# Seams between the two stages of a four-layer spectral network: copies inside SBUF in place of the way through DRAM, no barriers, and group loads one pair earlier

## What is computed

```python
h = einsum('bhwi,ic->bhwc', x, fc0_w) + fc0_b          # then channels first
for l in range(4):
    xf = rfft2(h)
    top = einsum('bixy,ioxy->boxy', xf[:, :, :16, :16], w1[l])
    bot = einsum('bixy,ioxy->boxy', xf[:, :, -16:, :16], w2[l])
    sc = irfft2(of)                                    # of: top and bot in a spectrum of zeros
    y = sc + einsum('bihw,oi->bohw', h, pw_w[l]) + pw_b[l]
    y = (y - mean) * rsqrt(var + eps) * gamma[l] + beta[l]   # mean and var over images and pixels
    h = gelu(y)
h = gelu(h @ fc1_w + fc1_b); out = h @ fc2_w + fc2_b   # per pixel
```

## Time and profile before

| | us |
|---|---|
| median of 3 runs | 4336.68 (4324.19 to 4337.49) |
| profiled execution | 4346.47 |
| its span | 4344.7 |
| TensorE busy | 3227.5 (74%) |
| VectorE, ScalarE busy | 2415.4 (56%), 2244.2 (52%) |
| DMA | 798.68 MB, mean 184 GB/s |

### The profile page before, as it was taken

How to read it: one execution, slowest core, us unless ns; L and a number is a source line. 1 busy time by engine, 2 the same in 40 slices (tenths; PEclk the granted TensorE clock), 3 DMA queues, 4 the chain that set the end, 5 groups by cost and what they waited for, 6 DMA issues and landing times. The chain is left out here.

```text
span 4344.7 us, 119303 instructions
## 1 busy us (share of the span) xinstructions
PE 3227.5 (74%) x52804; PEld 1863.9 (43%) x52804; DVE 2415.4 (56%) x2474; ACT 2244.2 (52%) x2644; POOL 173.2 (4%) x249
## 2 busy tenths in 40 slices
PE   6758888885577677757577776755999996659777
PEld 4544444444444344435344343444444442543432
DVE  4545555554477677646577676744333332554556
ACT  3545566654466556546456555644666664222321
POOL 2013100000000000000000000000010102000000
PEclk8879999997799889878899888987999998669688
DMA  8857666667768878787678787887343331002042
GB/s 287 308 150 186 173 155 157 172 188 281 242 181 242 248 218 260 209 282 263 214 220 252 216 239 242 245 290 257 120 163 148 142 121 32 1 19 61 1 102 66
DMA packets 172143, 798.68 MB, mean 184 GB/s; under 512 B 31177, under 2 KB 37649, under 8 KB 122286
## 3 DMA queue, kind: packets, MB, share of 16 engines
q1 hardware_dynamic: 160796, 776.18, 58.8%
q0 software_dynamic: 7936, 13.65, 1.0%
q10 hardware_dynamic: 2898, 1.17, 0.1%
HBM read 448.68 MB, written 342.23 MB: 182 GB/s over the span
## 5 line engine op out<-in xcount | busy, mean ns | idle before, releaser
L828 PEld LDWEIGHTS bank<-fb,arena 64*64 64x64 f32 x16384 | 555.7, 196 | 540.1 <-issue 484.1
L828 PE MATMUL bank<-fb,arena 64*64 64x128 f32 x16384 | 619.7, 289 | 196.5 <-issue 140.7
L1045 ACT ACTIVATE arena<-bank 128x1024 f32<-128x1024 f32 x384 | 383.5, 1023 | 638.7 <-PE bank L973 423.7
L845 DVE TENSOR_TENSOR arena<-bank,arena 128x1024 f32<-128x1024 f32 x384 | 467.2, 1217 | 411.4 <-PE bank L828 408.8
L837 DVE STREAM_TRANSPOSE arena<-bank 128x1024 f32<-128x1024 f32 x256 | 318.8, 1245 | 535.7 <-PE bank L818 535.6
L1088 DVE STREAM_TRANSPOSE arena<-arena 128x1024 f32<-128x1024 f32 x384 | 458.3, 1212 | 134.2 <-ACT arena L1035 132.2
L818 PE MATMUL bank<-arena,ga 64*64 64x256 f32 x4096 | 308.8, 413 | 300.0 <-DMA arena<-spec_out 242.0
L973 PE MATMUL bank<-arena,wst 64*64 64x512 f32 x3072 | 414.7, 620 | 17.1 <-issue 11.1
L1052 ACT ACTIVATE arena<-arena 128x1024 f32<-128x1024 f32 x384 | 403.2, 1050 | 0.3
L1038 ACT ACTIVATE arena<-arena,shift,scale 128x1024 f32<-128x1024 f32 x256 | 316.3, 1236 | 129.2 <-DVE arena L845 127.0
L818 PEld LDWEIGHTS bank<-arena,ga 64*64 64x64 f32 x4096 | 167.3, 142 | 430.9 <-issue 359.3
(11 more groups left out here) (238 smaller groups left out, 3647.1 us busy)
## 6 DMA issues: line engine op xcount, KB each, us to landing
y_dram<-arena SPq DMA_DIRECT2D x384, 512.0 KB, 8.2
arena<-y_dram SPq DMA_DIRECT2D x96, 2048.0 KB
arena<-spec_in SPq DMA_DIRECT2D x32, 2048.0 KB, 10.0
spec_out<-arena SPq DMA_DIRECT2D x128, 512.0 KB, 8.2
arena<-in_w_modes SPq DMA_DIRECT2D x28, 2048.0 KB, 14.2
arena<-spec_out SPq DMA_DIRECT2D x112, 512.0 KB, 10.4
spec_in<-arena SPq DMA_DIRECT2D x96, 512.0 KB, 7.9
spec_in<-arena SPq DMA_DIRECT2D x8, 2048.0 KB, 12.5
```

The source lines that it names most:

```text
L828: mm = pe.matmul(hpx(bank[2 * s + i][CHAN[v], :])[:, :, j * S:(j + 1) * S], a2[p % 2][CHAN[i], :, v, 4 * T + j], hpx(fb2[CHAN[i], :]), sta ...
L845: dve.tensor_tensor(chunk(p, T), slot(s), chunk(p, T), ALU.add).then_inc(y_added, 1)
L1045: act.activation(chunk(p, T), slot(NEXT_SLOT[T]), ACT.Copy).then_inc(evicted, 1)
```

## The change

1. `load_piece(n)` becomes `load_piece(n + 1)`, with one piece more ahead of the loop: each quarter of a group is issued one pair earlier.
2. Mix to fused stage: the last chunk of group 0 is no more loaded from `spec_out` behind a barrier, but copied from `m_sb` into `grp[0]` by four DMAs of 64 KB, ahead of the chunk's stores. `turn` of the last half comes ahead of `cross`, and ScalarE's squares of that half wait for it. The arithmetic of the batch norm is cut: sums behind `rows` of pair 0's first half, variance and scale around `turn_rows` of pair 0.
3. Fused stage to mix: spectra of chunks 0 and 1 are loaded without the last group (1792 KB each) once their buffers are free: chunk 0 in SyncE's turn of pair 31, chunk 1 at the end. Their last group comes from `xs` by four DMAs of 64 KB each. The rotated copies of chunks 0 and 1 are made in two pieces, seven groups and the last.
4. The seven `phase_end` between the stages go; single waits on semaphores stand for them. The buffers of the mix are laid out so that `xs` lies on `m_sb[1]`.

```diff
@@ mix
+        def load_last_group(sp, c, src):
+            for v in range(2):
+                for ro in range(2):
+                    to = ro * C + v * HB
+                    sp.dma_start(s_sb[c][to:to + HB, NG - 1], src(c, v, ro)).then_inc(s_last_group, 16)
...
             def store(c):
                 sp.wait_ge(mixed_turned, (l * NCH + c) * 4 + 4)
...
+                for t in range(4):
+                    row = t % 2 * C + t // 2 * HB
+                    if c == NCH - 1:
+                        sp.dma_start(grp[0].rearrange("p (c v) b o -> p c (v b o)", v=2)[row:row + HB, c],
+                                     m_sb[c % 2][t * HB:(t + 1) * HB, 0].rearrange("p v x -> p (v x)")).then_inc(grp_loaded[0], 16)
...
-            for c in range(3):
-                load(c)
+            if first:
+                for c in range(2):
+                    load_spectra(sp, c, slice(0, NG - 1))
+                    if c > 0:
+                        sp.wait_ge(s_last_group, 64)
+                    load_last_group(sp, c, lambda c, v, ro: spec_in[c, ro * C + v * HB:ro * C + v * HB + HB, NG - 1])
+            else:
+                sp.wait_ge(spec_stored, l * (NG * 64) + 64)
...
+                sp.wait_ge(p_stored[0], l * (USES * 64))
...
+            load(2)
...
             def square(n, h):
-                if h == 0:
+                if n == NU - 1:
+                    act.wait_ge(mixed_turned, (l * NU + n + 1) * 2)
+                elif h == 0:
                     act.wait_ge(mix_done, l * NU + n + 1)
...
-            for n in range(NU):
+            for n in range(NU - 1):
                 cross(n, 1)
                 cross(n, 0)
                 turn(n)
...
+            turn(NU - 1)
+            cross(NU - 1, 1)
+            cross(NU - 1, 0)
@@ fused stage
+            def next_spectra(c, b, later):
+                sp.wait_ge(p_stored[b], l * (USES * 64) + USES * 64)
...
+                sp.wait_ge(squared, (l * NP + NP - later) * 4)
...
+                sp.wait_ge(spec_stored, l * (NG * 64) + (NG * 64))
...
+                load_spectra(sp, c, slice(0, NG - 1))
...
-            load_group(sp, l, 0, slice(NCH - 1, NCH))
+            load_piece(sp, l, 0)
             for n in range(NP + 2):
-                if n < NP:
-                    load_piece(sp, l, n)
+                if n + 1 < NP:
+                    load_piece(sp, l, n + 1)
                 if n > 1 and (n - 2) % Q == Q - 1:
+                    if n == NP + 1:
+                        sp.wait_ge(hdft_turned, (l * NP + NP) * 2)
...
+                        load_last_group(sp, 0, from_planes)
                     store_spectra((n - 2) // Q)
...
+                if n == NP - 1:
+                    next_spectra(0, 1, 2)
+            next_spectra(1, 3, 0)
+            sp.wait_ge(s_last_group, l * 128 + 192)
...
+            load_last_group(sp, 1, from_planes)
...
             turn_rows(dve, l, 0, 0, ROWS_SLOT[0])
+            vector_variance(dve, l)
             turn_rows(dve, l, 0, 1, ROWS_SLOT[1])
+            vector_scale(dve, l)
@@ program of each engine
             sync_mix(sp, 0, True)
-            phase_end(sp, 2)
             sync_fuse(sp, 0, True)
-            phase_end(sp, 3)
...
```

More of the change, by code:

```diff
@@ L623, in tensor_mix, with tensor_sums @@
                     product(n + 1)
+        def tensor_sums(pe, l):
             pe.wait_ge(bn_step, l * BN_STEPS + 4)
             pe.sem_inc(waited[pe.engine], 1)
-            pe.matmul(bank[0][:, 0:2], half[:], bn[:, 8:10], start=True, stop=True).then_inc(bn_sum, 1)
+            pe.matmul(bank[4][:, 0:2], half[:], bn[:, 8:10], start=True, stop=True).then_inc(bn_sum, 1)
         def scalar_mix(act, l, first):
@@ L633, in rotate @@
                     act.wait_ge(mix_done, (l * NCH + c) * 2 - 2)
-                act.activation(r_sb[c % 2][0:C], s_sb[c % 3][C:P], ACT.Copy, scale=-1.0).then_inc(imag_up, 1)
+                else:
+                    if c == 0 and not first:
+                        act.wait_ge(p_stored[2], l * (USES * 64))
+                        act.sem_inc(waited[act.engine], 1)
+                    act.activation(r_sb[c][0:C, 0:NG - 1], s_sb[c][C:P, 0:NG - 1], ACT.Copy, scale=-1.0)
+                    act.wait_ge(s_last_group, l * 128 + c * 64 + 64)
+                    act.sem_inc(waited[act.engine], 1)
+                gs = slice(NG - 1 if c < 2 else 0, NG)
+                act.activation(r_sb[c % 2][0:C, gs], s_sb[c % 3][C:P, gs], ACT.Copy, scale=-1.0).then_inc(imag_up, 1)
             def copy_product(n, h):
@@ L664, in scalar_mix @@
                     rotate(n // 2 + 1)
-            act.wait_ge(bn_step, l * BN_STEPS + 7)
-            act.sem_inc(waited[act.engine], 1)
-            act.activation(bn[:, 14:15], bn[:, 13:14], ACT.Sqrt).then_inc(bn_root, 1)
+            scalar_root(act, l)
         BN_STEPS = 12
@@ L676, in rotate @@
                     dve.wait_ge(mix_done, (l * NCH + c) * 2 - 2)
-                dve.tensor_copy(r_sb[c % 2][C:P], s_sb[c % 3][0:C]).then_inc(real_down, 1)
+                else:
+                    if c == 0 and not first:
+                        dve.wait_ge(p_stored[2], l * (USES * 64))
+                        dve.wait_ge(squared, l * (NP * 4) - 4)
+                        dve.sem_inc(waited[dve.engine], 1)
+                    dve.tensor_copy(r_sb[c][C:P, 0:NG - 1], s_sb[c][0:C, 0:NG - 1])
+                    dve.wait_ge(s_last_group, l * 128 + c * 64 + 64)
+                    dve.sem_inc(waited[dve.engine], 1)
+                gs = slice(NG - 1 if c < 2 else 0, NG)
+                dve.tensor_copy(r_sb[c % 2][C:P, gs], s_sb[c % 3][0:C, gs]).then_inc(real_down, 1)
             def cross(n, h):
@@ L706, in turn @@
                     dve.sem_inc(waited[dve.engine], 1)
-                dve.wait_ge(s_squared, (l * NU + n) * 2 + 2)
+                if n == 2 and not first:
+                    dve.wait_ge(spec_stored, l * (NG * 64) + 64)
+                    dve.sem_inc(waited[dve.engine], 1)
+                if n < NU - 1:
+                    dve.wait_ge(s_squared, (l * NU + n) * 2 + 2)
+                else:
+                    dve.wait_ge(mix_done, l * NU + n + 1)
                 dve.sem_inc(waited[dve.engine], 1)
@@ L1002, in h_dft @@
                 mm.then_inc(hdft_done, 1)
+            pe.wait_ge(mixed_turned, (l * NU + NU - 1) * 2)
+            pe.sem_inc(waited[pe.engine], 1)
             rows_of(0, 0)
+            tensor_sums(pe, l)
             rows_of(0, 1)
@@ L1032, in gelu @@
                 n = l * NP + p
+                if p == 0 and T == 0:
+                    act.wait_ge(bn_step, l * BN_STEPS + 12)
+                    act.sem_inc(waited[act.engine], 1)
                 if first:
@@ L1100, in h_turn @@
                 dve.wait_ge(hdft_done, l * NP + p + 1)
+                if p == 0:
+                    dve.wait_ge(mixed_stored[1], l * (NCH * 32) + NCH * 32)
+                    dve.sem_inc(waited[dve.engine], 1)
                 if q == 0:
@@ L1271, in gelu @@
             def gelu(p, T):
+                if p == 0 and T == 0:
+                    act.wait_ge(bn_step, L * BN_STEPS)
                 act.wait_ge(y_added, A + p * 4 + T + 1)
@@ L1310, in vector_last @@
             turn_rows(dve, l, 0, 0, 0)
+            vector_variance(dve, l)
             turn_rows(dve, l, 0, 1, 0)
+            vector_scale(dve, l)
+            dve.memset(win, 0.0).then_inc(fc2_ready, 1)
+            dve.wait_ge(fc2_ready, 1)
+            dve.tensor_copy(win[:, 31:32], fc2[:]).then_inc(fc2_ready, 1)
             for n in range(NP):
```

88 lines of the change are left out of this document (42 added, 46 removed).

## The result

| | before | after |
|---|---|---|
| median of 4 runs, us | 4337.1 (4324.2 to 4345.8) | 4150.8 (4147.5 to 4160.3) |
| profiled execution, its span | 4346.5, 4344.7 | 4160.3, 4158.5 |
| ratio | | 0.9576, 95% interval 0.9547 to 0.9606 |

The change wins 186 us, in the medians as in the two spans. Forecast were 231 us and 4106 (4050 to 4200). I divide both spans at the same events: a mix's first product, the issue of the group load in `ahead()`, the first `rows`, the last turn behind the forward transform (`h_turn`: L1104 before, L1202 after).

A forecast was written before the change was run, and what follows sets the result against it. No engine is full, so removing waits wins time until DMA is full. Pieces 147, mix to fused 38 and fused to mix 46 sum to 231 us, giving 4106 us from the 4336.7 us median; range 4050 to 4200.

The forecast's parts named there:

- Pieces: Fused stages: earlier pieces cover nearly all seven waits, steps fall to 19.6 us; 147 us won, bounds 91 and 167.
- SyncE's queue: Fused stages: a group's first piece now waits for `rows` of one pair later; costed at nothing.
- Mix to fused: Four seams: barrier and 256 KB load removed, the copy ends the wait next; 38 us won, bounds 15 and 50.
- The batch norm's return: Start of fused stages: variance and scale around `turn_rows` delay the second one by 0.7 us, four times, 3 us lost.
- Fused stage to mix: Three seams: landing, barrier, load and most rotation removed, queue late next; 46 us won, bounds 25 and 60.
- what the mixes gave back: Mixes start while 6 MB are still under way, so gaps may fall there; 2 us a seam lost.
- DMA is the bound: Rival, layers 1 and 2: steps stay at 22 us, waiting at L845 in place of L818; 4248 us, chance 0.08.
- Gaps vanish: Rival, layers 1 and 2: with DMA evened out, every step is a quiet one of 17.5 us; 3988 us, chance 0.04.
- Late copies: Rival, mix to fused seams: copies held up behind pair loads, or slow, win nothing; 4144 us, chance 0.08.
- slower: Rival, layers 1 and 2: full DMA queues multiply TensorE's gaps, steps grow to 25.9 us; 4498 us, chance 0.03.

The follow-up runs named there:

- copies_first: Changed kernel with the loads of pairs 0 and 1 issued behind the last chunk's four copies at the four mix-to-fused seams; 4129.7 us (0.9523).
- the pieces alone: Kernel before with only the group's pieces issued one pair earlier, barriers and ways through DRAM kept at the seams; 4215.8 us (0.9715).

## Why the prediction was right, and where it was too high

- **Pieces, 147 us forecast, 110.9 measured.** The step "covers nearly all of the seven waits" holds: they are gone. "I take 19.6 us for every step" failed: it is 20.1 in layer 1 and 20.4 in layer 2. I had named the reason (no pause in which the backlog drains, gaps of TensorE) but sized it at 0.3 us a step. In layer 1 the removed 69.7 us of waits came back with 15 us of longer gaps (52.8 to 68.3), in layer 2 the 72.5 with 20 (59.1 to 79.1), which leaves 54.3 and 52.5 against 52.1 and 55.5 measured. By the steps, layer 1 won 48.4 us in the 27 and 8.0 on the first border, where I had 62 and 9, and lost 3.0 ahead of the first turn (below) and 1.3 behind the 27. Those 3.0 I had in no term of the pieces. The share came out at 0.86, not 0.88. SyncE's queue, costed at nothing, shows no wait for `rows`; layer 3 gained nothing, as said (3.5 us lost there with the tail). Two readings were off without weight: the quickest of the 27 steps is 17.2 us, not 17.5, and steps of 19.3 give 80 us a layer, not 81.
- **Mix to fused, 38 forecast, 33.6 measured.** "What ends the wait next is the copy" is right, and so is the order of the queue (copies_first: 9.8 us). Landing takes 19.5 us from the group load, 18.1 forecast: 8.3 to 9.0 us a seam won in place of 10. Layer 0 won 7.7 in place of 11. The batch norm's return, 0.7 us a layer in the forecast, shows as 0.5 us from `rows` to `spectral` (5.34 before, 5.88 after), but the first addition stands 8.1 us behind `rows` in place of 6.6, and the first turn 44.7 and 45.1 us in layers 1 and 2, where the kernel before has 41.7 and 40.7 and the pieces alone 41.8 and 41.6. So the earlier start gives back 3.0 and 4.4 us there, and 0.7 was too little; how much of it is the batch norm's no run separates. In the table this cost lies in the fused stages.
- **Fused stage to mix, 46 forecast, 47.2 less what the mixes gave back.** Won 13.9, 20.0, 13.3 us a seam in place of 17, 21.7, 14.6: I let the copies be issued at once, and they take 7.8 us. The mixes of layers 1 to 3 grew by 2.3, 1.5 and 4.6 us, 8.3 in sum against 6; that of layer 0 fell by 4.8, but in the second profile of the same kernel it was 160.4, 3.7 more than before, so those 4.8 are chance.
- **Rivals.** "DMA is the bound", with a wait at the addition in place of the old one, fell (1.0 us of it). What it missed is that DMA can bind without a wait for data: halving `y_dram` wins 155 us. "Gaps vanish" named the right lever and the wrong direction: the change makes DMA fuller, so gaps grow; they shrink only when data is taken away or sent in another order. "Late copies" and "slower" fell.

## What to carry to other kernels

Of a seam with a barrier and a way through DRAM take away both, or expect little: they run side by side, and each alone kept half or more of the gain from coming. A barrier charges every engine with the queue of the engine that issues the transfers; count that engine's issue time, not only the last landing, and look for a branch behind it that each engine could have taken earlier by itself. And when a long unrolled TensorE program runs beside DMA at over 0.8, look for gaps that nothing releases, hold their distances against the period of the program and their ends against the packets of the instruction queue, and spread the transfers before you look for another wait to remove.

## What was not expected of the hardware

- Blocks of TensorE's program arrive late when DMA is full: up to 4.5 us for one in layer 1 and 5.2 in layer 2, at distances of multiples of some 247 matmuls and weight loads, and 68 and 79 us a layer. The block itself passes in about 1 us; it starts late.
- The branch back to the start of a loop cost TensorE, VectorE, ScalarE and SyncE 5.6 to 7.0 us each with data under way (run with the barriers) and 3.5 to 3.7 us without (kernel before): the first packets of instructions started 3.5 us behind it there and 0.8 us here.
- The issue of four DMAs of 64 KB takes 7.8 us behind 1.8 MB of spectra, 4 MB of weights and 2 MB of stores on the same queue, and 2.5 us without the weights. The bytes ahead do not decide it alone: at the other seam, behind 6 MB of group and pairs that had just been issued, it takes 2.65 us.
- A copy within SBUF is served in the queue's order: with 4 MB ahead of it (two pairs) it lands 18 us behind its issue, without them 9.2 us (issued 1122.03, `rows` at 1131.21).
- A mix that starts 5 to 7 us sooner ends no sooner (two of three end 2 and 5 us later), at an unchanged DMA share (0.82 in layer 1's mix).
